# A token tower on one core: the order of each engine's program written out for all pairs

## The reference

```python
# 1. tokens: embedding, windowed PCA features, fusion, layer norm
combined = concat([emb[ids], (window3(pca[ids] * mask) / length) @ proj_w + proj_b])
h = layernorm(combined @ fus_w + fus_b) * ln_g + ln_b
# 2. linear attention, 16 heads of 16, keys = the normalised stream itself
X = layernorm(h); Q = rms(X @ Wq.T) * qw; V = rms(X @ Wv.T) * vw
W = cumsum(einsum('blhd,blhe->blhde', X, V), axis=1)
h = h + einsum('blhd,blhde->blhe', Q, W)
# 3. feed-forward of width 1024, activations and weights quantised (int8 steps, ternary weights)
X = quantise(layernorm(h)) @ ternary(w1).T
h = h + quantise(silu(depthwise_conv3(X) + conv_b)) @ ternary(w2).T
```

## Time and profile before

| what | us |
|---|---|
| median of three runs | 291.01 (289.68 to 291.11) |
| profiled execution | 293.25 |
| its span, first to last instruction | 291.5 |
| VectorE busy | 199.6 |
| TensorE busy (matmul) | 200.8 |
| ScalarE busy | 159.5 |
| POOL busy | 106.6 |

### The profile page before, as it was taken

One profiled execution on the slowest core, in us unless ns is written; L12 is line 12 of the kernel. 1 busy time (PEld: TensorE's weight loads), 2 busy tenths in 40 slices (PEclk: granted clock), 3 DMA queues, 4 the chain that ended last, 5 costly groups with the idle time before them and its releaser, 6 DMA issues.

```text
span 291.5 us, 4867 instructions
## 1 busy us (share of the span) xinstructions
PE 200.8 (69%) x1456; PEld 147.2 (50%) x1456; DVE 199.6 (68%) x555; ACT 159.5 (55%) x282; POOL 106.6 (37%) x225
## 2 busy tenths in 40 slices
PE   0459377078429969776985997698589767676624
PEld 0126345056328648554854775485467556344312
DVE  2834518945691893898589489858937987785671
ACT  0201050014713795687597668759774975996902
POOL 8102821043105437436424734642513324333300
PEclk9999659559956987996898799689859978665757
DMA  6970010101102012103111220311112024011011
GB/s 152 329 274 2 0 36 9 29 2 36 32 6 62 14 36 38 36 17 57 38 36 39 40 73 15 57 38 36 41 36 74 0 52 48 12 36 37 2 36 36
DMA packets 29403, 14.23 MB, mean 49 GB/s; under 512 B 15616, under 2 KB 28098, under 8 KB 29378
## 3 DMA queue, kind: packets, MB, share of 16 engines
q1 hardware_dynamic: 27888, 13.28, 19.0%
q10 hardware_dynamic: 1490, 0.65, 0.8%
HBM read 5.51 MB, written 2.10 MB: 26 GB/s over the span
## 4 chain that ended last, share of the span: by engine, by line
PE 35%; DVE 27%; issue 11%; ACT 10%; SPq 9%; DMA 7%; DVEq 1%; ACTq 0%
PE PO L750 7%; PE PA L687 6%; SPq L306 5%; DMA feat<-sd 4%; PE PY L791 4%; PE PA L699 3%; SPq L283 3%; PE PH L765 3%; PE PS L709 3%; PE PO L744 3%; ACT w_s L546 2%; ACT tap L540 2%; DVE ST L1069 2%; PE PS L732 2%; DMA mask_b<-in_mask_dram 2%
## 5 line engine op out<-in xcount | busy, mean ns | idle before, releaser
L436 POOL TENSOR_TENSOR hid<-hid,tap 128x508 f32<-128x508 f32 x32 | 40.9, 1282 | 42.3 <-DVE hid L1127 42.3
L765 PE MATMUL PH<-xsT,w1q 128*128 128x256 f16 x256 | 44.8, 306 | 16.0 <-DVE hid L1127 15.9
L537 ACT ACTIVATE hid<-PH,cb_s,cw_x 128x256 f32<-128x256 f32 x64 | 35.9, 561 | 19.6 <-PE PH L765 19.2
L765 PEld LDWEIGHTS PH<-xsT,w1q 128*128 128x128 f16 x256 | 24.4, 105 | 33.4 <-issue 25.3
L732 PE MATMUL PS<-QP,KM 128*128 128x256 f32 x128 | 35.2, 403 | 5.9 <-DVE ST L1069 3.2
L1127 DVE SCALAR_TENSOR_TENSOR hid<-PH,cw_x,hid 128x254 f32<-128x254 f32 x64 | 30.3, 477 | 12.6 <-ACT tap L540 12.2
L546 ACT ACTIVATE w_s<-hid 128x512 f32<-128x512 f32 x32 | 36.0, 1138 | 5.4 <-POOL hid L436 5.3
L750 PE MATMUL PO<-VD,ST 128*64 128x32 f32 x512 | 35.8, 266 | 0.0
L750 PEld LDWEIGHTS PO<-VD,ST 128*64 128x64 f32 x512 | 34.1, 187 | 0.0
L732 PEld LDWEIGHTS PS<-QP,KM 128*128 128x128 f32 x128 | 23.0, 198 | 14.6 <-issue 12.3
L540 ACT ACTIVATE tap<-PH,cw_x 128x256 f32<-128x256 f32 x64 | 29.9, 468 | 0.0
(11 more groups left out here) (186 smaller groups left out, 400.3 us busy)
## 6 DMA issues: line engine op xcount, KB each, us to landing
QP<-QT SPq DMA_DIRECT2D x32, 64.0 KB, 2.1
VD<-Vn SPq DMA_DIRECT2D x32, 64.0 KB, 2.1
out_dram<-y SPq DMA_DIRECT2D x8, 256.0 KB, 2.2
ids_b<-in_ids_dram SPq DMA_DIRECT2D x4, 256.0 KB, 5.7
mask_b<-in_mask_dram SPq DMA_DIRECT2D x4, 256.0 KB, 6.9
w_s<-in_w1T_dram SPq DMA_DIRECT2D x1, 1024.0 KB, 10.0
w_s<-in_w2T_dram SPq DMA_DIRECT2D x1, 1024.0 KB, 12.1
fusw_s<-in_fusw_dram ACTq DMA_DIRECT2D x2, 256.0 KB, 5.2
```

Source lines behind the costliest of these rows:

```text
L436: nc.gpsimd.tensor_tensor(part, part, tap[:, c % 2, :, :, 0:T - 1], ALU.add).then_inc(tap0_ok, 1)
L537: nc.scalar.activation(hid[:, j, :, :].rearrange("p u t -> p (u t)"), hidps(j), ACT.Identity, bias=cb_s[:, j:j + 1], scale=cw_x[:, j, 1:2])
L765: ins = nc.tensor.matmul(hidps(j), w1q[:, k, j * 128:(j + 1) * 128], part[:, s, :, k, :], start=(n == 0), stop=(n == 2 * KC - 1))
```

## The change

The loop and `on` are gone. Each engine's stages are written out one by one for all eight pairs, in an order that differs from place to place. No instruction is new; `split_parity` is called once for each of its two instructions, `weight_sums` of ScalarE becomes `weight_sum(0)` and `weight_sum(1)`, and `ternary_weights` becomes `ternary_w1` and `ternary_w2`. `projb_x` is copied ahead of `features(0)`. SP's token and weight loads keep their place ahead of everything else. The core of the diff (the middle of the long lists is left out):

```diff
-            for i in range(NP + 5):
-                on(spread_v, i - 2)
-                on(std_row, i - 1)
-                on(turn_xs, i - 3)
-                on(spread_q, i - 1)
-                on(store, i - 5)
-                if i == 0:
-                    load_ffn()
+            std_row(0); spread_q(0); std_row(1); spread_v(0); std_row(2); spread_q(1); spread_v(1); spread_q(2)
+            turn_xs(0); std_row(3); spread_v(2); spread_q(3); std_row(4); turn_xs(1); spread_v(3); spread_q(4)
+            std_row(5); turn_xs(2); spread_v(4); spread_q(5); store(0); std_row(6); spread_v(5); turn_xs(3)
+            spread_q(6); std_row(7); store(1); turn_xs(4); spread_q(7); spread_v(6); turn_xs(5); store(2)
+            spread_v(7); turn_xs(6); store(3); store(4); turn_xs(7); store(5); store(6); store(7)
...
-                on(add_tap, i - 4, 1)
...
-                on(weigh_roots, i - 1)
+            variance0(0); variance1(0); variance0(1); weigh_roots(0); variance1(1); variance0(2); variance1(2)
+            residual(0, 0); residual(0, 1); inv_root2(0); weigh_roots(1); variance0(3); variance1(3); residual(1, 0)
+            residual(1, 1); add_tap(0, 0); inv_root2(1); weigh_roots(2); variance0(4); add_tap(0, 1); variance1(4)
...
-                on(split_parity, i - 1)
...
-                if i == 2:
-                    weight_sums()
+            def weight_sum(n):
+                act.wait_ge((ld_w1, ld_w2)[n], 16)
+                wait(act, wabs_ok, n)
+                nc.scalar.activation(w_junk, (w1_s, w2_s)[n][:, :], ACT.Abs, accum_out=wabs[:, n:n + 1]
+                                     ).then_inc(wabs_ok, 1)
+
+            weight_sum(0); take_tables(); square_q(0); take_q(0); split_parity(0, 0); split_parity(0, 1)
+            square_v(0); take_x0(0); weight_sum(1); take_h(0, 0); take_h(0, 1); split_parity(1, 0); take_q(1)
...
+            taps(1, 7); widen_hid(0, 0); widen_hid(0, 1); square_q(5); take_q(5); split_parity(5, 0)
+            split_parity(5, 1); taps(2, 0); square_v(5); silu(1, 3); normalise2(3, 0); taps(2, 1); normalise2(3, 1)
+            take_h(5, 0); taps(2, 2); take_h(5, 1); taps(2, 3); silu(2, 0); take_x0(5); taps(2, 4); xs_high(3, 0)
+            taps(2, 5); xs_high(3, 1); taps(2, 6); silu(2, 1); silu(2, 2); taps(2, 7); square_q(6)
...
-            table_k_q()
-            for i in range(NP + 5):
-                on(gram, i)
...
+            gram(0); fold(0); table_k_q(); gram(1); fold(1); table_x_v(); keys_queries(0); sum_q(0); values(0)
+            scores(0, 0, 0); scores(0, 0, 1); weight_sums(); scores(0, 1, 0); gram(2); state(0); fold(2)
+            keys_queries(1); scores(0, 1, 1); attend(0, 0, 0); values(1); sum_q(1); attend(0, 0, 1); attend(0, 1, 0)
+            attend(0, 1, 1); scores(1, 0, 0); scores(1, 0, 1); gram(3); state(1); fold(3); scores(1, 1, 1)
+            keys_queries(2); scores(1, 1, 0); attend(1, 1, 1); values(2); sum_q(2); attend(1, 0, 0); scores(2, 0, 0)
+            scores(2, 0, 1); attend(1, 0, 1); attend(1, 1, 0); hidden(0, 0); hidden(0, 1); scores(2, 1, 0)
...
+            turn_max(0); hidden(1, 3); values(4); hidden(1, 4); attend(3, 0, 1); hidden(1, 5); attend(3, 1, 1)
+            scores(4, 0, 1); attend(3, 0, 0); attend(3, 1, 0); spread_scale(0); hidden(1, 6); hidden(1, 7)
+            scores(4, 1, 1); gram(6); scores(4, 0, 0); fold(6); state(4); keys_queries(5); scores(4, 1, 0); down(0)
+            hidden(2, 0); values(5); hidden(2, 1); sum_q(5); hidden(2, 2); attend(4, 0, 0); attend(4, 1, 1)
+            attend(4, 1, 0); hidden(2, 3); turn_max(1); attend(4, 0, 1); hidden(2, 4); scores(5, 0, 0)
+            scores(5, 0, 1); hidden(2, 5); gram(7); hidden(2, 6); state(5); fold(7); spread_scale(1); hidden(2, 7)
+            keys_queries(6); scores(5, 1, 0); hidden(3, 0); hidden(3, 1); scores(5, 1, 1); values(6)
...
-            features(0)
             dve.wait_ge(ld_emb, 16)
             nc.vector.tensor_copy(projb_x[:, :, 1:1 + V], projb_s[:, :, None].to_broadcast([128, KC, V])
                                   ).then_inc(projb_ok, 1)
+            features(0)
...
-            def ternary_weights():
...
+            def ternary_w1():
...
+            def ternary_w2():
...
-            for i in range(NP + 5):
-                on(mask_scores, i - 2, 1, 1)
...
+            features(1); products(0); take_stats(0); products(1); take_tables(); take_stats(1); features(2)
+            mean_q(0); sum_v(0); mean_v(0); scale_mean_v(0); root_seed(0); root_half(0); root_square(0, 0)
+            root_error(0, 0); root_step(0, 0); mask_scores(0, 0, 0); root_square(0, 1); root_error(0, 1)
+            root_step(0, 1); root_square(0, 2); root_error(0, 2); root_step(0, 2); scale_v(0); mask_scores(0, 1, 0)
+            products(2); mask_scores(0, 0, 1); take_stats(2); mask_state(0); features(3); mask_scores(0, 1, 1)
+            sum_v(1); mean_v(1); mean_q(1); scale_mean_v(1); root_seed(1); root_half(1); root_square(1, 0)
+            root_error(1, 0); root_step(1, 0); root_square(1, 1); root_error(1, 1); root_step(1, 1)
+            root_square(1, 2); root_error(1, 2); scale_out(0, 0); root_step(1, 2); scale_out(0, 1); scale_v(1)
+            moments2(0, 0); variance2(0, 0); moments2(0, 1); products(3); mask_scores(1, 0, 1); variance2(0, 1)
+            mask_state(1); take_stats(3); mask_scores(1, 0, 0); shift_x(0); mask_scores(1, 1, 1); ternary_w1()
+            maxima_x(0); step_x(0); inv_step_x(0); mask_scores(1, 1, 0); quantise_x(0, 0); quantise_x(0, 1)
+            sum_v(2); xs_low(0, 0); mean_v(2); mean_q(2); scale_mean_v(2); xs_low(0, 1); root_seed(2); root_half(2)
+            root_square(2, 0); ternary_w2(); root_error(2, 0); root_step(2, 0); mask_scores(2, 0, 0)
+            root_square(2, 1); scale_out(1, 0); root_error(2, 1); mask_scores(2, 0, 1); root_step(2, 1); conv(0, 0)
+            root_square(2, 2); root_error(2, 2); scale_out(1, 1); root_step(2, 2); conv(0, 1); scale_v(2)
+            moments2(1, 0); moments2(1, 1); variance2(1, 0); variance2(1, 1); products(4); conv(0, 2); conv(0, 3)
...
+            hid_scale(1); step_x(3); scale_out(4, 1); inv_step_x(3); root_step(5, 2); quantise_x(3, 0); scale_v(5)
+            conv(2, 4); quantise_x(3, 1); xs_low(3, 0); conv(2, 5); products(7); xs_low(3, 1); mask_scores(5, 0, 0)
+            take_stats(7); moments2(4, 0); conv(2, 6); mask_scores(5, 0, 1); variance2(4, 0); moments2(4, 1)
+            quantise(1, 0); conv(2, 7); variance2(4, 1); mask_state(5); quantise(1, 1); hid_max(2, 0)
...
+            mask_scores(7, 1, 0); hid_max(4, 1); finish(3, 1); hid_max2(4); conv(5, 6); scale_out(7, 0); conv(5, 7)
+            hid_top(4); hid_step(4); hid_scale(4); moments2(7, 0); scale_out(7, 1); conv(6, 0); variance2(7, 0)
+            quantise(4, 0); conv(6, 1); moments2(7, 1); quantise(4, 1); variance2(7, 1); quantise(4, 2)
...
+            finish(6, 1); hid_max2(7); hid_top(7); hid_step(7); hid_scale(7); quantise(7, 0); quantise(7, 1)
+            quantise(7, 2); quantise(7, 3); finish(7, 0); finish(7, 1)
```

More of the change, by code:

```diff
@@ new lines, in _ @@
+            moments2(1, 0); moments2(1, 1); variance2(1, 0); variance2(1, 1); products(4); conv(0, 2); conv(0, 3)
+            shift_x(1); take_stats(4); mask_state(2); maxima_x(1); step_x(1); mask_scores(2, 1, 1); inv_step_x(1)
+            conv(0, 4); mask_scores(2, 1, 0); quantise_x(1, 0); quantise_x(1, 1); hid_max(0, 0); xs_low(1, 0)
+            sum_v(3); mean_v(3); mean_q(3); conv(0, 5); scale_mean_v(3); xs_low(1, 1); root_seed(3); root_half(3)
+            root_square(3, 0); scale_out(2, 0); root_error(3, 0); scale_out(2, 1); root_step(3, 0)
@@ new lines, in _ @@
+            mask_scores(3, 0, 0); root_square(3, 1); root_error(3, 1); root_step(3, 1); conv(0, 6)
+            root_square(3, 2); root_error(3, 2); root_step(3, 2); conv(0, 7); scale_v(3); mask_scores(3, 0, 1)
+            moments2(2, 0); products(5); conv(1, 0); conv(1, 1); take_stats(5); mask_scores(3, 1, 1); moments2(2, 1)
+            variance2(2, 0); hid_max(0, 1); variance2(2, 1); hid_max2(0); mask_scores(3, 1, 0); shift_x(2)
+            mask_state(3); hid_top(0); conv(1, 2); maxima_x(2); mean_q(4); hid_step(0); step_x(2); conv(1, 3)
@@ new lines, in _ @@
+            inv_step_x(2); hid_scale(0); sum_v(4); mean_v(4); quantise_x(2, 0); scale_mean_v(4); root_seed(4)
+            root_half(4); quantise_x(2, 1); root_square(4, 0); root_error(4, 0); root_step(4, 0); root_square(4, 1)
+            mask_scores(4, 0, 1); root_error(4, 1); conv(1, 4); root_step(4, 1); root_square(4, 2); conv(1, 5)
+            root_error(4, 2); scale_out(3, 0); root_step(4, 2); scale_out(3, 1); scale_v(4); quantise(0, 0)
+            quantise(0, 1); products(6); xs_low(2, 0); xs_low(2, 1); mask_scores(4, 0, 0); take_stats(6)
@@ new lines, in _ @@
+            mask_scores(5, 1, 0); shift_x(4); conv(3, 0); mask_scores(5, 1, 1); quantise(1, 2); conv(3, 1); sum_v(6)
```

(14 more changed lines are left out.)

203 lines of the change are left out of this document (80 added, 123 removed).

## The result

The new kernel takes 0.8845 of the time before (95% interval 0.8789 to 0.8902), some 33.6 us less. The median of all its runs is 260.42 us (258.08 to 263.3); some of them ran beside a lower TensorE clock, and the ratio leaves those out, and with them one execution of the kernel before of 860.82 us. The profiled execution took 258.2 us with a span of 256.5; forecast were 255.5 and 256.

What follows compares the result with a forecast made beforehand. Waits between engines bound the kernel, neither VectorE nor TensorE being full. Front 87, middle 155 (134.8 / 0.87) and tail 14.2 gave span 256; plus 1.75 less 2.24, 255.5 us, range 243 to 271.

Steps and rivals of the forecast that it cites:

- The front: Start up to the end of scale_v(2): ends at 87 us, not 105.05, 18 us gained, bounds 12 and 23.
- The even part: Middle pairs: keys_queries(5) follows scale_v(4) by some 3.7 us in place of 7.2, 3.5 us of cover.
- The chain through SP's queue: Between scale_v and keys_queries: spread_v's transfers delay std_row's; with std_row(g+1) ahead, neither's issues lie between.
- The share of VectorE: VectorE's busy share in the even part: 0.87 in place of 0.787, as scale_out's wait falls from 15.7 to about 3 us.
- the waits for taps and `sum_q`: VectorE's waits in conv and mean_q over the even part: left as they are, 8.6 and 2.8 us.
- The work of VectorE: VectorE's busy time left after scale_v(2): 131.81 us plus about 3.0, 134.8, with no instruction added or taken away.
- the contention at POOL's end: POOL's operations lengthened by VectorE's SBUF reads: counted as 0, at the outside 6 us, which would make the sum 261.5.
- Rival (b): Nearly full: the three engines mesh, VectorE at 0.95, span 243, time 242.7; chance 0.14 for below 246.
- The tail: From the last hid_max to the last store: a chain of one pair, the same in both kernels, 14.2 us.
- The clock: TensorE's granted clock, 0.62 to 0.87 of 2.4 GHz in the stretches: may rise, but no gain counted.

Runs made afterwards that it cites:

- a8_tap_quarter: New kernel with POOL's add_tap cut in four instructions of a quarter each: 0.8520 of the kernel before.
- b1_row_first: Kernel before with one exchange in SP's loop, std_row(i-1) ahead of spread_v(i-2): 0.9682 of the kernel before, 9.3 us less.
- a5_row_last: New kernel with SP's std_row(g+1) put back behind spread_v(g) for g = 0 to 6: 1.0215 of the kernel before.
- a2_tap_split: New kernel with POOL's add_tap cut in two instructions of half the width: 0.8678 of the kernel before, 0.985 of the new kernel.

## Why the prediction was right, point by point

- **The front.** Forecast 87, measured 84.15. The first `keys_queries` came later than forecast (37.76, not 35.9: 3.1 us lost, just outside the bounds of 0 and 3; at the other pace of TensorE that `a8_tap_quarter` shows, 0.5), the second and third about as forecast (52.09 and 66.53 for 53.1 and 68.8), the third `scale_v` at 83.47 for 86.3. The way there was as told: `features` and the weight sums off the path.
- **The even part.** The chain through SP's queue is gone, as forecast, 3.1 us in place of 7.2 with 3.7 forecast. `b1_row_first` shows that the queue alone was worth 9 us in the old order, and `a5_row_last` that the new order rests on it.
- **The share of VectorE.** Forecast 0.87, measured 148.84 / 158.49 = 0.94, held time included. I had left the waits for taps and `sum_q` as they were, 11.4 us; they too went, down to 2.3 and 1.1 over the whole span. The size was off: VectorE's idle time in this stretch was forecast at 20 us and measured at 9.7. The new list has other stages in front of these two waits as well, as in front of `scale_out`; which of its places took them away, no single run shows.
- **The work of VectorE.** Forecast 134.8 us after `scale_v(2)`, measured 148.84. This is the step that failed: "No instruction is added or taken away", and from it "So the work stays at rows 1". The prediction saw the contention at POOL's end (0.81 in place of 0.27 us), priced it at 0 to 6 us, and did not ask what it does to VectorE. The Trainium skill's "GPSIMD Engine Reference", section 1, says that VectorE instructions in a two-port mode or with two SBUF inputs contend with GpSimd. For those with two SBUF inputs the trace agrees (`xs` 0.48 to 1.31 us); in which mode the held `tensor_scalar` ran, no run here shows. The runs add that the engine that starts second pays, until the other's instruction ends, and that in the new order this is mostly VectorE.
- **The errors cancel.** After the front 134.8 / 0.87 = 155 was forecast, 158.5 measured: 14 us more work, 10.5 us less idle time. With the forecast work and the measured idle time it would have been 144.5. The 3.5 us too many are then offset by a front 2.9 us shorter and a tail 0.3 shorter than forecast. So the span is right to 0.5 us for a reason that is half luck. Rival (b), 243, was the nearer one for the waits: 84.15, 144.45 and 13.86 make 242.5, and the runs of the new kernel with the small `add_tap` have spans of 242.0 to 247.5. The time is off by a little more than the span, 258.2 for 255.5, since the forecast took off 2.24 us by which the profiled execution of the kernel before was longer than its median; in the new kernel the profiled execution was hardly longer than the next (258.08).
- **The tail**, 14.2 forecast, 13.86 measured, unchanged as told.
- **The clock.** I had counted no gain. TensorE's stood at 0.97 in the even part, and its busy time after the front fell from 134.62 to 123.30 us for the same work. No run separates what this gave. That it was little has this for it: two runs of the new kernel at mean granted clocks of 0.855 and 0.900 have spans of 256.3 and 256.5 us.

## What to carry to other kernels

A loop over one body, however well tuned, gives each stage one place for all steps; look in the chain for a transfer or a small stage that waits only for its place in a queue, and move that first: here an exchange of two lines on SP gave 9 us, more than a fourth of what the whole rewriting did. An order written out stage by stage is tight: one queue out of order cost more than all that the rewriting had gained. And when stages change places, ask which of them will now run at the same time on two engines, and which starts first: busy time is not a constant of the program, and here long POOL instructions were worth cutting in two (1.5%) once VectorE was the bound.

## What the hardware showed unexpectedly

VectorE's `xq` (`tensor_scalar` from SBUF) and `xs` (two SBUF inputs) took up to 1.0 us more than their usual 0.34 and 0.48 when a POOL instruction had begun before them; when they had begun first, it was POOL's `add_tap` that took 1.45 us in place of 1.27. Operations with a PSUM source kept their time in the new order (`conv` 470 ns after, 477 before; `mask_scores` 679 and 683), and so did the reductions. The other forms were not tried one by one. Cutting the POOL instruction in two cost POOL 0.16 us a cut (5.2 us for 32 in `a2_tap_split`), and gave VectorE 5 us back.
